# The second sequence's attention result in chunks 1 to 6: scaled by ScalarE and added to x by GpSimd, instead of by VectorE from PSUM

## What is computed

```python
# attention with a distance decay, per sequence
weights = einsum('bsd,btd->bst', xn @ W + b, xn)
weights = exp(tanh(weights * lw)) * off_diag          # lw = 1/|s-t|
attn = (weights / (sum(weights) + EPS)) @ xn
# mixture of 8 experts, two per token, and a shared expert; hidden size 176
scores = sigmoid(xn @ gate_w.T); sel = top_k(scores + expert_bias, 2)
routed = sum over sel of relu(scores[sel] * xn @ w_up[sel].T)**2 @ w_down[sel].T
shared = relu(xn @ shared_w_up.T)**2 @ shared_w_down.T
out = x + attn + routed + shared
```

## Time and profile before

| what | value |
|---|---|
| median of 3 runs | 118.19 us (117.75 to 118.61) |
| span of the profiled execution, first to last instruction | 116.0 us |
| PE busy | 110.6 us (95%) |
| DVE busy | 101.1 us (87%) |
| ACT busy | 89.5 us (77%) |
| POOL busy | 69.6 us (60%) |
| granted TensorE clock, mean | 1.000 |

### The profile page before, as it was taken

The page is one execution under the profiler, slowest core; times in us unless marked ns, Lnnn a source line. Parts: engine busy times, 40 slices in busy tenths (PEclk is TensorE's granted clock), DMA queues, the critical chain, the costliest instruction groups (busy, mean ns, idle before and its releaser), DMA issues.

```text
span 116.0 us, 2804 instructions
## 1 busy us (share of the span) xinstructions
PE 110.6 (95%) x914; PEld 85.1 (73%) x914; DVE 101.1 (87%) x319; ACT 89.5 (77%) x139; POOL 69.6 (60%) x119
## 2 busy tenths in 40 slices
PE   3988999999999999999999999999999999999991
PEld 3965558787868776869578776879588767859790
DVE  6969989999998989989998989988998689989751
ACT  4444799987788987969799687969699687897760
POOL 6538993499999499635973499636972520613200
PEclk9999999999999999999999999999999999999999
DMA  4999105886776759892849939593949648687882
GB/s 97 319 263 331 68 0 100 78 167 126 139 145 108 195 100 193 54 245 48 167 82 220 124 70 179 103 163 79 172 84 219 124 84 164 117 216 136 131 208 90
DMA packets 47965, 16.56 MB, mean 143 GB/s; under 512 B 45008, under 2 KB 45904, under 8 KB 47952
## 3 DMA queue, kind: packets, MB, share of 16 engines
q1 hardware_dynamic: 47376, 15.44, 66.0%
q0 software_dynamic: 288, 0.72, 3.2%
q10 hardware_dynamic: 288, 0.23, 1.0%
HBM read 3.84 MB, written 2.10 MB: 51 GB/s over the span
## 4 chain that ended last, share of the span: by engine, by line
PE 94%; DVE 1%; issue 1%; POOL 1%; ACT 0%; DVEq 0%; POOLq 0%
PE out_ps L1029 16%; PE h_ps L980 15%; PE side L957 12%; PE dots L936 11%; PE out_ps L1017 6%; PE out_ps L1011 4%; PE small L921 4%; PE side L970 4%; PE small L893 4%; PE out_ps L1059 4%; PE small L877 3%; PE h_ps L993 2%; PE small L902 1%; PE side L912 1%; PE side L921 1%
## 5 line engine op out<-in xcount | busy, mean ns | idle before, releaser
L698 DVE SCALAR_TENSOR_TENSOR gated<-h_ps,gates 128x1408 bf16<-128x1408 f32 x28 | 45.2, 1615 | 4.7 <-PE h_ps L980 4.4
L505 ACT ACTIVATE hidden<-gated 128x1408 bf16<-128x1408 bf16 x30 | 41.1, 1378 | 2.6 <-DVE gated L698 1.6
L1029 PE MATMUL out_ps<-downT,hiddenT 128*128 128x128 bf16 x341 | 22.8, 219 | 0.0
L1029 PEld LDWEIGHTS out_ps<-downT,hiddenT 128*128 128x128 bf16 x341 | 20.8, 98 | 2.3 <-issue 0.6
L980 PE MATMUL h_ps<-upT,xnTb 128*128 128x512 bf16 (+1 forms) x84 | 21.3, 362 | 0.0
L276 POOL TENSOR_SCALAR xn<-x_sb,meanvar,rstd 128x128 f32<-128x128 f32 x26 | 20.4, 795 | 0.6
L957 PEld LDWEIGHTS side<-xn,probs 128*128 128x128 f32 x120 | 15.1, 191 | 1.5 <-issue 0.5
L957 PE MATMUL side<-xn,probs 128*128 128x129 f32 x120 | 15.8, 274 | 0.0
L936 PE MATMUL dots<-projT,xnT 128*128 128x256 f32 x60 | 15.4, 379 | 0.0
L309 POOL TENSOR_SCALAR_AFFINE_SELECT probs<-probs 128x256 f32<-128x256 f32 x16 | 6.5, 408 | 12.7 <-ACT probs L462 12.6
L980 PEld LDWEIGHTS h_ps<-upT,xnTb 128*128 128x128 bf16 x84 | 7.2, 98 | 9.4 <-issue 3.2
(11 more groups left out here) (117 smaller groups left out, 178.9 us busy)
## 6 DMA issues: line engine op xcount, KB each, us to landing
x_sb<-in_x SPq DMA_DIRECT2D x7, 256.0 KB, 9.1
out_y<-final SPq DMA_DIRECT2D x7, 256.0 KB, 2.5
hiddenT<-hidden SPq DMA_TRANSPOSE x31, 3.6
upT<-in_up POOLq DMA_DIRECT2D x1, 352.0 KB, 7.5
downT<-in_down POOLq DMA_DIRECT2D x1, 352.0 KB, 8.4
late_sb<-in_late SPq DMA_DIRECT2D x1, 192.0 KB, 3.6
x_sb<-in_x ACTq DMA_DIRECT2D x1, 128.0 KB, 2.4
x_sb<-in_x SPq DMA_DIRECT2D x1, 128.0 KB, 2.5
```

The costliest lines, as they stand in the source:

```text
L505: a.activation(hidden[:, t, :], gated[:, t, :], ACT.Square).then_inc(squared, 1)
L698: v.scalar_tensor_tensor(out=gated[:, t, :].rearrange("p (e h) -> p e h", e=E), in0=h_ps[:, 0:NH].rearrange("p (e h) -> p e h", e=E), scal ...
L1029: last = t_.matmul(out_at(c, t), hiddenT[:, c % 2, t, j, :], downT[:, j, :], start=(t == 0 and j == 0 and c < LAST), stop=((t >= 2 or c == ...
```

## The change

ACT takes over the scaling of the second sequence's result, and POOL the addition of x, in chunks 1 to 6. Chunk 0 did so already, and the last chunk stays with DVE.

- A new buffer `scaled_second` (two slots) takes ACT's result, so that `scale_attention(1)` no longer waits for `second_resid`.
- ACT: `scale_second(c)` for c = 1 stands behind `square(1, 1)` and ahead of `take_pair(2)`; in the loop (c = 2 to 6) behind `square(c, 1)` and ahead of `take_proj(f)`. It waits for `attend_norm(c, 1)` and for POOL's addition of chunk c - 2.
- POOL: `add_second_x(1)` stands behind `add_x(1)`; in the loop (c = 2 to 6) it stands behind `make_gates(f)` and ahead of `square_shared(c)` and the two masks.
- DVE: `attend(1)` and the loop's `attend(c)` go. `attend(LAST)` stays, with a wait on `final_ready`.
- Those who waited for `attn_taken` now wait for `second_resid` (DVE's `finish(c, 1)`) or `second_scaled` (PE's `shared_main(c)` for c = 1 to 6).

```diff
         scaled = sb("scaled", [P, 2, 2, D])
+        scaled_second = sb("scaled_second", [P, 2, 2, D])
         resid = sb("resid", [P, 2, TILES, D])
...
 
-            def add_second_x():
-                pool.wait_ge(second_scaled, 1)
-                g.tensor_tensor(resid[:, 0, 2:4, :], scaled[:, 1, :, :], x_sb[:, 0, 2:4, :], ALU.add
+            def add_second_x(c):
+                pool.wait_ge(second_scaled, c + 1)
+                wait(pool, final_ready, 2 * (c - 1))
+                g.tensor_tensor(resid[:, c % 2, 2:4, :], scaled_second[:, c % 2, :, :], x_sb[:, c, 2:4, :], ALU.add
                                 ).then_inc(second_resid, 1)
...
             square_first_chunk_end()
-            add_second_x()
+            add_second_x(0)
             mask(1, 1)
...
             add_x(1)
+            add_second_x(1)
             square_shared(1)
...
                     make_gates(f)
+                if c < LAST:
+                    add_second_x(c)
                 square_shared(c)
...
                 act.wait_ge(attn_step, 2 * Q * c + 2)
-                if c == 1:
-                    act.wait_ge(second_resid, 1)
                 wait(act, first_resid, c - 1)
...
 
-            def scale_second():
-                act.wait_ge(attn_step, 4)
+            def scale_second(c):
+                act.wait_ge(attn_step, 2 * (Q * c + 1) + 2)
+                wait(act, second_resid, c - 1)
                 for t in range(2):
-                    last = a.activation(scaled[:, 1, t, :], attend_bank(0, 1)[:, t * (D + 1):t * (D + 1) + D],
+                    last = a.activation(scaled_second[:, c % 2, t, :],
+                                        attend_bank(c, 1)[:, t * (D + 1):t * (D + 1) + D],
                                         ACT.Identity, scale=rownorm[:, 1, t:t + 1])
...
             square(0, 2)
-            scale_second()
+            scale_second(0)
             relu_rest(2)
...
             square(1, 1)
+            scale_second(1)
             take_pair(2)
...
                 square(c, 1)
+                scale_second(c)
                 take_proj(f)
...
                 dve.wait_ge(attn_step, 2 * (Q * c + 1) + 2)
+                dve.wait_ge(final_ready, 2 * (c - 1))
                 for t in range(2):
...
                     dve.wait_ge(out_made, TILES * (c + 1))
-                    if c == 0:
-                        dve.wait_ge(second_resid, 1)
-                    else:
-                        dve.wait_ge(attn_taken, c)
+                    dve.wait_ge(second_resid, c + 1)
                 v.tensor_tensor(final[:, c, 2 * h:2 * h + 2, :], out_bank(h).rearrange("p (t d) -> p t d", t=2),
...
                 dve.wait_ge(out_made, TILES * LAST + (TILES if t == 2 else TILES - 1))
-                dve.wait_ge(attn_taken, LAST)
+                dve.wait_ge(attn_taken, 1)
                 v.tensor_tensor(final[:, LAST, t, :], out_at(LAST, t), resid[:, LAST % 2, t, :], ALU.add
...
             route_mark(2)
-            attend(1)
             finish(0, 0)
...
                 attend_norm(c, 1)
-                attend(c)
                 finish(o, 0)
...
                 elif c > 0:
-                    pe.wait_ge(attn_taken, c)
+                    pe.wait_ge(second_scaled, c + 1)
                 t_.matmul(shared_bank(c), supT, xnT[:, c % 4, :], start=True, stop=True).then_inc(sup_made, 1)
...
             def up_tile(c, t):
```

## The result

The changed kernel takes 118.52 us (median of 22 runs, 117.83 to 119.64) against 117.75 us for the kernel before (22 runs), a ratio of 1.0055 with a 95% interval from 1.0033 to 1.0077: 0.65 us slower (117.75 x 0.0055), between 0.4 and 0.9 us. The ratio is estimated from the fast executions alone, and two of the changed kernel's 22 were slow ones, so it isn't the quotient of the two medians (1.0065). The forecast was 0.9 us slower, within 1% and so as good as no change. The time lies inside the range and the side is right, but the loss is clear of no change: the interval reaches 0.22% to either side, far finer than the 1% that the prediction took for what a measurement can tell.

What follows compares the result with a forecast made beforehand. The prediction took PE to bound the loop. Its terms 0.16 + 0.40 + 0.40 = 0.96, taken as about 0.9 us, went onto the median of 118.19 us to give 119.1 us (+0.8%), range 118.0 to 120.5.

Steps and rivals of the forecast that it cites:

- `shared_main`: PE's load in k = 3 to 6 waits for ACT's scaled result, 0.04 us late each: 0.16 us, lower end 0.
- the masks of k = 3 to 6: POOL's addition delays mask(f, 0), so PE's attend(f, 0) comes late: 0.10 us in each of four stages, 0.40 us.
- the mask of k = 7: Last loop stage, smaller margin: late mask makes attend's matmul 0.48 us late, part comes back; 0.40 us, bounds 0.33 and 0.68.
- within 1%, like no change: Whole kernel: forecast of +0.8% lies within the 1% (1.2 us) that a measurement can tell from no change.
- PE bounds the loop, and DVE's relief is worth nothing: Loop: PE never stands still, so DVE's 0.6 us less work per chunk gains 0 on the path.
- Where the relief would show: DVE's idle time ahead of gate(c, 0) was to grow from 0.57 to about 1.2 us.
- the 0.10 us that `up_by_bank(1)` was to give back: k = 7: PE's up_by_bank(1) takes 0.69 us against 0.59 elsewhere; 0.10 us of waiting for DVE's gates could absorb delay.
- Chunk 1, 0: ACT's scale_second(1) waits ahead of take_pair(2), DVE's marks come some 0.85 us later, idle time covers it: 0, at most 0.2.
- The slow rival: POOL's late mask paces PE at attend(f, 0) in every stage: slower by more than 1%, 119.9 to 120.6 us; chance 0.33.
- The rival in which DVE paces the loop: DVE sets the stage length, so its relief gives up to 3.0 us in five stages: 115.2 us; chance 0.06.
- The likeliest case: Whole kernel within 1%: the forecast of 119.1 us together with the mild case of 118.5 us; chance 0.61.

Runs made afterwards that it cites:

- the first two experiments: POOL's addition moved behind mask(f, 0) in the changed kernel: 0.9999; one more POOL addition ahead of square_shared(c) in the kernel before: 1.0071.
- the first experiment: The changed kernel with POOL's loop addition behind mask(f, 0) instead of ahead of square_shared(c): ratio to the kernel before 0.9999, 77.43 us between the loads.
- experiment 6: The changed kernel with POOL's addition behind mask(f, 0) and ACT's scale_second(c) behind take_proj(f): ratio to the kernel before 1.046, 4.84 us more between the loads.
- four kernels without the cost: Kernel before; changed kernel with POOL's addition behind mask(f, 0) or ahead of make_gates(f); kernel before with ACT's extra pair: 77.42 or 77.43 us between loads.

## Why the prediction came out as it did

In short: the wait was the right one, and three terms of the sum were mis-sized. `shared_main` cost 0 us instead of 0.16, the masks of k = 3 to 6 cost 0.26 us instead of 0.40, and the mask of k = 7 cost 0.49 us instead of 0.40. The common fault of the first two is that a late weight load was priced by its own lateness, or nearly so, while PE lost less than that. The step from this cost to "within 1%, like no change" failed too: it took 1.2 us for the least that can be told, and 0.65 us was told.

- **PE bounds the loop, and DVE's relief is worth nothing: right.** Shown by the first two experiments. Where the relief would show was wrong: I had it ahead of `gate(c, 0)`, from 0.57 to about 1.2 us. That idle time stayed at 0.57 us. The freed time stands ahead of `gate(c, 2)`, where DVE had no idle time in the kernel before, and `gate(c, 0)` keeps its old start relative to PE:

```profile
56.77 1.62 DVE L705 SCALAR_TENSOR_TENSOR gated<-h_ps,gates 128x1408 bf16<-128x1408 f32 x1 [0.48 <-PE h_ps L983]
```

- **`mask(f, 0)` in k = 3 to 6, 0.40 us: right mechanism, too large.** It measured 0.26 us, 0.06 to 0.07 per stage. The shift was 0.69 and the hand-over 0.05 us as worked out. What was over-sized is the price of a late load: 0.10 us was taken, and 0.11 us at the load made only 0.06 to 0.07 us. Why it makes that much, with the first matmul on time, isn't shown. The Trainium skill's rule that was weighed there (TensorE: Matmul & The Clock Gate, section "Architectural detail: the array is 16x 32x32, not 1x 128x128"), that a matmul can begin before its weight load has completed, fits what the trace shows: the first matmul starts 0.05 us behind the start of a load, in k = 7 0.01 us behind it, and one such load lasts 0.19 us (28.07). By that rule the term would have been 0.1 us; the measurement lies between the rule's price and mine.
- **`mask(f, 0)` in k = 7, 0.40 us: 0.49 us.** The delay of what follows the group was 0.49 us, where 0.48 was worked out (for the first matmul, which was 0.39 us late; the longer group made the rest). The step that failed is the 0.10 us that `up_by_bank(1)` was to give back. Its 0.69 us, part of which I took for a wait for DVE's gates, are there unchanged in the changed kernel (103.48 to 104.17), where the gates end at 103.03, 0.45 us ahead of it. What they are isn't shown; the page calls the load's idle time behind them "issue", in both kernels.
- **`shared_main(c)`, 0.16 us: 0.** ACT's pair ends at 56.34, as forecast to the hundredth, and the load of `shared_main` starts at 56.41, where PE's own sequence puts it (before: 56.35, with PE 0.06 us earlier). A hand-over of 0.05 us fits in, with 0.02 us to spare. In the first experiment, where PE isn't behind, the load was 0.02 us late and the matmul on time. So the failed step is that the 0.04 us at the load were put into the sum, although the prediction itself had noted that the matmul couldn't start earlier anyway (its lower bound, 0). The cover is thin all the same, and experiment 6 shows what lies behind it.
- **Chunk 1, 0: right.** ACT waited 1.86 us for the reciprocal and DVE's marks 0.79 us for ACT, as worked out, and PE's load of `attend(2, 0)` starts 8.42 us after that of `attend(1, 1)` in both kernels (36.50 - 28.08 and 36.49 - 28.07).
- **The sum.** 0.16 + 0.40 + 0.40 = 0.96 was forecast and rounded down to 0.9; 0 + 0.26 + 0.49 = 0.75 was measured between the loads. Two terms were 0.16 and 0.14 us too large and one 0.09 us too small, so part of the nearness is luck. The times themselves, 119.1 forecast and 118.52 measured, lie further apart because the forecast started from a median of three runs, 118.19, and 22 runs gave 117.75. The slow rival named the right wait and had it at the wrong end of its bounds: it needed 0.15 us per stage and got 0.06. The rival in which DVE paces the loop is refuted. The likeliest case was left at "within 1%", like no change, and the 0.55% is a real loss.

## What to carry to other kernels

When work moves to an engine with idle time, its share of busy time says nothing; what counts is the first instruction behind the new one that the bounding engine waits for, and the margin between that result and its use. Here POOL was busy for 60% of the time, the margin was 0.60 us, the new instruction delayed what stands behind it by 0.69, and putting it two places later, or one earlier into an existing wait, made it free. Look at the last stage by itself: here the bounding engine had less to do ahead of the same wait, the margin was 0.20 us instead of 0.60, and one stage of five made two thirds of the loss.

## What was not expected of the hardware

The spans of kernels that lose nothing in the loop differ by up to 0.5 us, and the traces place that in the first 8 us, in PE's warm-up of 20 equal matmuls and the few that follow it. The kernel before:

```profile
1.90 4.64 PE L1059 MATMUL out_ps<-ident 128*128 128x128 f32 x20 [1.90 <-POOL ident L256]
```

and the first experiment, whose code up to that point is the same:

```profile
1.90 4.06 PE L1062 MATMUL out_ps<-ident 128*128 128x128 f32 x20 [1.90 <-POOL ident L257]
```

In the first, no matmul of the warm-up takes less than 421 ns. In the second they take 421 ns at first as well, and from 5.6 us on 275 ns, while the granted clock of the stretch from 5.0 to 6.3 us reads 1.00, the upper of its two levels (2.4 GHz), in both. So these matmuls get short at a different moment from one execution to the next, and because PE bounds the kernel, the 0.5 us stay to the end (116.0 and 115.5 us). Which event sets the moment was not tested. It is a good reason to measure small differences between two instructions of the bounding engine: between the two loads, four kernels without the cost agree within 0.01 us, where the times of one kernel's runs scatter by about 1 us.
